# Two Mamba-2 layers and a quantised MLP on one core: the first convolution tap moves from GpSimd to ScalarE, with new instruction orders in the scan

## The chip, the core and the metric

The kernel runs on 1 core of one Trainium2 chip. The metric is the device time of one execution in microseconds; the time before is the median of 3 runs. The core has five instruction streams that run side by side and wait for each other by semaphores: TensorE (PE), VectorE (DVE), ScalarE (ACT), GpSimd (POOL) and SyncE (SP). Each runs its own instructions strictly in the order of the code.

## The reference

The input is x, 8 sequences of 1024 tokens of 256 channels. After a normalisation come two Mamba-2 layers with residuals, then x is added, normalised again, and three blocks of a quantised MLP with LoRA follow. The change touches the Mamba layers alone:

```python
zxbcdt = u @ in_w.T                       # u: layer norm of h; z 512, xBC 640, dt 8 columns
z, xBC, dt = split(zxbcdt)
dt = softplus(dt + dt_bias)
xBC = silu(causal_depthwise_conv(xBC, conv_w, 4 taps) + conv_b)
xh, B, C = split(xBC)                     # 512, 64, 64
dA = exp(dt * -exp(A_log))
state = dA * state + (dt * x) B^T ; y = state C      # per head, token after token
y = (y + D * xh) * silu(z)
y = y * rsqrt(mean(y * y) + eps) * rms_w
h = h + y @ out_w.T
```

## The kernel before

**Tiling.** A layer is worked off in 16 items; an item n is a chunk of 128 tokens of 4 of the 8 sequences, so 512 tokens. `over_items` (twice per layer by hand, then a hardware loop over pairs, then two by hand) runs the function `step(n, ...)` of each engine for the 32 items of both layers. The convolution works on tiles of 128 channels x 512 tokens in float32; there are five of them (`QCONV`), in the order B/C tile first, then four tiles of x, numbered i = 0 to 4. The scan within a chunk is done with matrix products: decays between tokens (`decays`, `exp_decay`, `weigh`, in four pieces k = 0 to 3, two blocks of tokens by half the heads), scores of C and B, the output within the chunk (`within`) and from the carried state (`carried`), and the new state (`new_state`).

**Staging.** In step(n) the engines finish item n and make the front part of item n + 1 (projections, convolution, softplus, its pieces k = 0 and 1) and the layer norm and transposes of item n + 2. No planner runs: the order of work on each engine is the order of the calls in its `step`, written out by hand, and each call begins with waits for semaphores that count instructions of other engines.

**A convolution tile i passes four engines.** TensorE's `project_conv(i)` (L502) makes it in a PSUM bank: two banks (`front`) alternate, so tile i needs that tile i - 2 is through. ScalarE's `raw_conv(i)` (L806) copies it with its bias to `xpad` in SBUF, behind a halo of 3 tokens which VectorE's `set_halo` (L1270) puts there. GpSimd's `first_tap(i)` (L1019) multiplies `xpad`, shifted by three tokens, with the weight of tap 0 into `xc`. VectorE's `convolve(i, 0..2)` (L1286) adds the other three taps; the first of them, `convolve(i, 0)`, waits for the first tap (`tap0`), each other one for the one before. ScalarE's `silu_conv(i)` (L824) ends it.

**The work around it.** ScalarE: `exp_decay(k)` (L851, Abs then Exp over two banks `dbank`), `exp_carry(pair)` (L864, Exp over the two `mix` banks), `softplus` (L797, with a table load for Ln), `norm` (L777), `square(t)` (L868), `silu_z(t)` (L846), `keep_b`, `double_c` (two DMAs on ScalarE's queue). VectorE: `layer_moments` (L1106), `bias_dt` (L1209), `weigh(k)` (L1309), `scale_x(b)` (L1318, frees the `mix` banks of `turn_x`), `scale_c(pair)` (L1323), `skip(t)` (L1329), `split_sums` (L1226, which makes the parts that `turn_cum` transposes), `decay_operands` (L1256), `first_operands` (L1264), `rest_u` (L1205), `mean_square` (L1346), `finish` (L1350). TensorE: `decays(k)` waits for `weigh(k - 1)`, since there is one pair of decay banks; `carry(0)` waits for all four `scale_x`, `carry(1)` for `scale_c(0)`; `outputs(0)` for `weigh(3)`; `project_conv(4)` for `convolve(2, 2)`; `turn_cum` (L522) for `convolve(4, 2)`; `project_z(t)` (L530) for `silu_z(t - 2)`. GpSimd: `to_end` (L1028), `gate(t)` (L1014, waits for `skip(t)`), `decay_state`, `layer_norm` (L983), `add_squares`, `second_operands` (L991), `norm_residual` (first layer alone), two `rsqrt`.

## Time and profile before

| | before |
|---|---|
| median of 3 runs | 1781.3 us (1776.38 to 1782.0) |
| profiled execution | 1781.56 us |
| its span, first to last instruction | 1779.8 us |
| TensorE busy | 1637.6 us, 92% |
| VectorE busy | 1369.8 us, 77% |
| ScalarE busy | 1268.5 us, 71% |
| GpSimd busy | 1183.8 us, 67% |
| mean granted TensorE clock | 0.978 |

The Mamba layers take the first 1370 us or so, the MLP the rest. Shares of busy time are means over parts with different limits, so the profile is read by the timeline: each row of it is an instruction or several of one kind in a run, with its start from the span's start, its length (of the whole run, where it is several), the engine, the line, what it writes and reads, and, in brackets, how long the engine had been idle before it and what released it. TensorE instructions overlap in their records. On the other engines a following instruction that depends on nothing may start about 0.1 us before the end of the one before.

### The profile page before, as it was taken

What the parts mean: (1) busy time and instruction counts of PE and PEld (TensorE: products, weight loads), DVE (VectorE), ACT (ScalarE), POOL (GpSimd) and SP (SyncE); (2) the same over time, 40 slices, a digit from 0 to 9 for tenths busy, and PEclk for the clock granted to TensorE, in tenths of its full rate; (3) what the DMA queues carried; (4) which work ended last, traced back from release to release, by engine and by line L of the source; (5) the groups of instructions that cost most, each with busy time, mean ns of one, the idle gap of its engine ahead of it and who ended that gap; (6) DMA issues with size and microseconds to landing.
All of it is one profiled execution on the core that took longest, in us unless ns stands there. A gap on an engine that the chain in (4) does not pass through costs nothing. (4 is left out here: it accounts for less than half of the span.)

```text
span 1779.8 us, 35344 instructions
## 1 busy us (share of the span) xinstructions
PE 1637.6 (92%) x12440; PEld 1290.7 (73%) x12440; DVE 1369.8 (77%) x2941; ACT 1268.5 (71%) x1999; POOL 1183.8 (67%) x1022
## 2 busy tenths in 40 slices
...
GB/s 162 19 48 43 43 41 41 56 62 41 41 41 47 41 42 36 48 43 43 43 53 64 41 41 41 47 41 41 29 160 32 99 1 143 1 109 35 36 13 48
DMA packets 87045, 91.67 MB, mean 52 GB/s; under 512 B 4928, under 2 KB 82224, under 8 KB 86960
## 3 DMA queue, kind: packets, MB, share of 16 engines
...
## 5 line engine op out<-in xcount | busy, mean ns | idle before, releaser
L1025 POOL TENSOR_TENSOR L_xc<-L_xpad,L_vec 128x512 f32<-128x512 f32 x160 | 166.2, 1039 | 313.2 <-ACT L_xpad L814 237.2
L498 PE MATMUL L_front<-L_uhi,L_whi 128*128 128x512 f32 x568 | 243.8, 429 | 9.2 <-DVE L_xc L1302 4.7
L666 PE MATMUL L_mix<-L_wo,L_yg 128*128 128x256 f32 x1024 | 240.7, 389 | 0.0
L853 ACT ACTIVATE L_dbank<-L_dbank 128x1024 f32<-128x1024 f32 x128 | 129.2, 1009 | 143.9 <-PE L_dbank L559 143.1
L498 PE MATMUL L_front<-L_uhi,L_wlo 128*128 128x512 f32 x568 | 226.4, 399 | 0.0
L498 PE MATMUL L_front<-L_ulo,L_whi 128*128 128x512 f32 x568 | 225.7, 397 | 0.0
L1315 DVE TENSOR_TENSOR L_m<-L_dbank,L_gm 128x1024 f32<-128x1024 f32 x128 | 156.3, 1221 | 84.2 <-ACT L_dbank L855 84.2
L666 PEld LDWEIGHTS L_mix<-L_wo,L_yg 128*128 128x128 f32 x1024 | 196.5, 195 | 28.7 <-issue 0.9
L1017 POOL TENSOR_TENSOR L_yg<-L_yg,L_sz 128x512 f32<-128x512 f32 x128 | 176.8, 1392 | 37.7 <-DVE L_yg L1331 37.7
L1036 POOL TENSOR_TENSOR L_wx<-L_dtx,L_decay 128x512 f32<-128x512 f32 x120 | 124.1, 1045 | 94.5 <-DVE L_dtx L1320 94.5
L1777 POOL TENSOR_TENSOR M_alo<-M_hT,M_ahi 128x512 fp32r<-128x512 f32 x96 | 129.3, 1362 | 46.3 <-ACT M_ahi L1710 46.3
L814 ACT ACTIVATE L_xpad<-L_front,L_pbias 128x512 f32<-128x512 f32 x156 | 106.6, 684 | 63.4 <-PE L_front L498 62.8
L498 PEld LDWEIGHTS L_front<-L_uhi,L_whi 128*128 128x128 f32 x568 | 108.0, 190 | 59.8 <-DVE L_xc L1302 19.3
L849 ACT ACTIVATE L_sz<-L_front,L_pbias 128x512 f32<-128x512 f32 x128 | 87.5, 685 | 85.8 <-PE L_front L498 82.2
L855 ACT ACTIVATE L_dbank<-L_dbank 128x1024 f32<-128x1024 f32 x128 | 129.0, 1008 | 3.4
L617 PE MATMUL L_ybank<-L_m,L_dtx 128*64 128x128 f32 x2048 | 129.4, 280 | 1.3 <-DVE L_m L1315 1.3
L1784 POOL TENSOR_TENSOR M_alo<-M_g,M_ahi 128x512 fp32r<-128x512 f32 x96 | 126.5, 1337 | 3.7 <-ACT M_ahi L1734 3.6
L1002 POOL TENSOR_TENSOR L_sq<-L_sq 128x512 f32<-128x512 f32 x96 | 124.6, 1298 | 3.7 <-ACT L_sq L870 0.5
L498 PEld LDWEIGHTS L_front<-L_uhi,L_wlo 128*128 128x128 f32 x568 | 108.0, 190 | 25.8
L617 PEld LDWEIGHTS L_ybank<-L_m,L_dtx 128*64 128x64 f32 x2048 | 113.6, 140 | 15.1 <-issue 12.0
L1296 DVE SCALAR_TENSOR_TENSOR L_front<-L_front,L_vec,L_xc 128x512 f32<-128x512 f32 x156 | 117.6, 754 | 5.2 <-POOL L_xc L1025 5.1
L498 PEld LDWEIGHTS L_front<-L_ulo,L_whi 128*128 128x128 f32 x568 | 108.6, 191 | 17.3
...
## 6 DMA issues: line engine op xcount, KB each, us to landing
...
```

The source lines that it names most:

```text
L498: last = nc.tensor.matmul(to[:, :], ww[:, kd, tile * P:(tile + 1) * P], a[:, kd, :], start=i == 0, stop=i == len(passes) - 1)
L617: nc.tensor.matmul(ybank[t % 2][half, b * P:(b + 1) * P], dtx[:, b, 2 * t + odd, :], m[:, b, 2 * t + odd, :], start=b == 0, stop=False, sk ...
L666: last = nc.tensor.matmul(mix[1 - s][:, (b % 2) * DM:(b % 2 + 1) * DM], yg[:, t, b * P:(b + 1) * P], wo[layer][:, t, :], start=t == 0, sto ...
L853: nc.scalar.activation(dbank[:, :, :], dbank[:, :, :], ACT.Abs).then_inc(d_abs, 1)
L855: nc.scalar.activation(dbank[:, :, :], dbank[:, :, :], ACT.Exp, scale=-1.0).then_inc(d_exp, 1)
L1002: nc.gpsimd.tensor_tensor(sq[:, 0, :], sq[:, 0, :], sq[:, t, :], ALU.add).then_inc(sq_added, 1)
L1017: nc.gpsimd.tensor_tensor(yg[:, t, :], yg[:, t, :], sz[:, t, :], ALU.mult).then_inc(y_gated, 1)
L1025: nc.gpsimd.tensor_tensor(xc[p][:, q, :].rearrange("p (b i) -> p b i", b=NB), xpad[:, q, :, 0:P], vector(layer, "conv_w", q * TAPS, 1).uns ...
L1036: nc.gpsimd.tensor_tensor(wx[:, b, :, :], dtx[:, b, :, :], decay[p][:, b, :].unsqueeze(2).broadcast_to([P, NH, HD]), ALU.mult).then_inc(wx ...
L1315: nc.vector.tensor_tensor(m[:, at, heads, :], dbank[:, :, :].rearrange("p b (h i) -> p b h i", i=P), gm[:, at, :].unsqueeze(2).broadcast_t ...
L1777: nc.gpsimd.tensor_tensor(alo[u][:, kd, :], hT[u][:, kd, :], ahi[u][:, kd, :].bitcast(F32), ALU.subtract).then_inc(h_lo, 1)
L1784: nc.gpsimd.tensor_tensor(alo[u][:, kd, :], g[u][:, kd, :], ahi[u][:, kd, :].bitcast(F32), ALU.subtract).then_inc(g_lo, 1)
```

## The change

The multiplication by the weight of tap 0 is no longer done on GpSimd. `first_tap` becomes an activation of ScalarE (Identity with a scale of one value per partition, SBUF to SBUF), called right behind `raw_conv` of the same tile, in the prologue too. It waits for the raw copy to be complete, and for tile 0 for `set_halo`. The other engines' waits stay. All four `step` functions get a new order:

- TensorE: `decays(2)` and `turn_dt` come before `result(n-1, 1)`; `project_conv(1)` and `decays(3)` before `turn_x(1)`; `carry(1)` behind `project_conv(3)`; `square_sums` behind `result(n, 0)`.
- ScalarE: `exp_decay(3)` before `keep_b`; `softplus` before `raw_conv(3)`; `norm` and `square(0)`, `square(1)` behind the second and third `silu_conv`; `square(2)` before `silu_z(1)`; `exp_sums` and `keep_halo` change places.
- GpSimd: `decay_state` before the gates, `layer_norm` behind `gate(1)`, `second_operands` behind the first `add_squares`, the `rsqrt` of the result before `norm_residual`.
- VectorE: `set_halo` behind `layer_moments`; `bias_dt` and `weigh(n, 2)` before `convolve(0, 0)`; `convolve(1, 2)` before `scale_c(0)`; `finish_dt` before `convolve(3, 0)`; `decay_operands` before `skip(2)`; `first_operands` before `add_state`; `mean_square` behind `rest_u`.

The diff (leading spaces cut):

```diff
@@ -713,26 +713,25 @@
     more, more2 = follows(n, 1), follows(n, 2)
     if more:
         project_conv(n + 1, 0)
+    spread_factors(n, 0)
+    turn_x(n, p, 0)
+    if more:
+        turn_dt(n + 1)
+    decays(n, 2)
     if follows_any(n):
         result(n - 1, layer_of(n, layer, -1), 1)
-    spread_factors(n, 0)
-    turn_x(n, p, 0)
-    decays(n, 2)
-    if more:
-        turn_dt(n + 1)
+    if more:
+        project_conv(n + 1, 1)
+    decays(n, 3)
     turn_x(n, p, 1)
     turn_x(n, p, 2)
-    if more:
-        project_conv(n + 1, 1)
     turn_x(n, p, 3)
     turn_b(n, p)
     carry(n, 0)
-    decays(n, 3)
     if more:
         project_conv(n + 1, 2)
+        project_conv(n + 1, 3)
     carry(n, 1)
-    if more:
-        project_conv(n + 1, 3)
     outputs(n, p, 0)
     spread_factors(n, 1)
     spread_factors(n, 2)
@@ -756,13 +755,13 @@
         scores(n + 1, 1 - p)
     if more2:
         turn_u(n + 2, p)
+    result(n, layer, 0)
+    if not more:
+        square_sums(n)
     if more:
         square_sums(n)
     if starts_layer(n + 2):
         fold_bias(layer_of(n, layer, 2))
-    result(n, layer, 0)
-    if not more:
-        square_sums(n)
     if more:
         decays(n + 1, 1)
     if more2:
@@ -821,6 +820,15 @@
     nc.scalar.activation(halo[g][:, :, :, :].rearrange("p q b i -> p (q b) i"),
                          xpad[:, :, :, P:P + HALO].rearrange("p q b i -> p (q b) i"), ACT.Copy).then_inc(halo_kept, 1)
 
+def first_tap(n, layer, p, i):
+    q = QORDER[i]
+    act.wait_ge(x_raw, QCONV * n + i + 1)
+    if i == 0:
+        act.wait_ge(halo_set, n + 1)
+        wait(act, y_skip, T * (n - 1))
+    nc.scalar.activation(xc[p][:, q, :].rearrange("p (b i) -> p b i", b=NB), xpad[:, q, :, 0:P], ACT.Identity,
+                         scale=vector(layer, "conv_w", q * TAPS, 1)).then_inc(tap0, 1)
+
 def silu_conv(n, layer, p, i):
     q = QORDER[i]
     act.wait_ge(taps, 3 * QCONV * n + 3 * i + 3)
@@ -891,6 +899,7 @@
     softplus(n)
     for i in range(QCONV):
         raw_conv(n, 0, p, i)
+        first_tap(n, 0, p, i)
     keep_halo(n, p)
     for i in range(QCONV):
         silu_conv(n, 0, p, i)
@@ -914,52 +923,56 @@
         raw_conv(n + 1, layer1, 1 - p, 0)
     exp_decay(n, 2)
     if more:
+        first_tap(n + 1, layer1, 1 - p, 0)
         raw_conv(n + 1, layer1, 1 - p, 1)
+        first_tap(n + 1, layer1, 1 - p, 1)
+    exp_decay(n, 3)
     keep_b(n)
     exp_carry(n, 0)
-    exp_decay(n, 3)
     if more:
         raw_conv(n + 1, layer1, 1 - p, 2)
+        first_tap(n + 1, layer1, 1 - p, 2)
     exp_carry(n, 1)
     round_mlp(n, 0)
     if more:
+        softplus(n + 1)
         raw_conv(n + 1, layer1, 1 - p, 3)
-        softplus(n + 1)
+        first_tap(n + 1, layer1, 1 - p, 3)
         silu_conv(n + 1, layer1, 1 - p, 0)
         raw_conv(n + 1, layer1, 1 - p, 4)
-    if more2:
-        norm(n + 2, p)
-    if more:
+        first_tap(n + 1, layer1, 1 - p, 4)
         silu_conv(n + 1, layer1, 1 - p, 1)
+        silu_conv(n + 1, layer1, 1 - p, 2)
+        double_c(n + 1, 1 - p)
     square(n, 0)
-    if more:
-        silu_conv(n + 1, layer1, 1 - p, 2)
     square(n, 1)
     round_mlp(n, 1)
     round_mlp(n, 2)
-    if more:
+    if more2:
+        norm(n + 2, p)
+    if more:
+        silu_conv(n + 1, layer1, 1 - p, 3)
+        silu_conv(n + 1, layer1, 1 - p, 4)
         silu_z(n + 1, layer1, 0)
-        silu_conv(n + 1, layer1, 1 - p, 3)
-        double_c(n + 1, 1 - p)
+    square(n, 2)
+    if more:
         silu_z(n + 1, layer1, 1)
-    square(n, 2)
-    if more:
         silu_z(n + 1, layer1, 2)
     square(n, 3)
     round_mlp(n, 3)
     round_mlp(n, 4)
     round_mlp(n, 5)
     if more:
-        silu_conv(n + 1, layer1, 1 - p, 4)
         silu_z(n + 1, layer1, 3)
         exp_decay(n + 1, 0)
+    if more2:
+        round_u(n + 2)
+    if more:
+        keep_halo(n + 1, 1 - p)
         exp_sums(n + 1, 1 - p)
     if starts_layer(n + 2):
         fold_weights(layer_of(n, layer, 2))
-    if more2:
-        round_u(n + 2)
-    if more:
-        keep_halo(n + 1, 1 - p)
+    if more:
         exp_decay(n + 1, 1)
 
 act.dma_start(raw[:, :, :], w["in_proj"][0].rearrange("(k p) n -> p k n", p=P)).then_inc(raw_in, 16)
@@ -1016,15 +1029,6 @@
     pool.wait_ge(z_done, T * n + T)
     nc.gpsimd.tensor_tensor(yg[:, t, :], yg[:, t, :], sz[:, t, :], ALU.mult).then_inc(y_gated, 1)
 
-def first_tap(n, layer, p, i):
-    q = QORDER[i]
-    pool.wait_ge(x_raw, QCONV * n + i + 1)
-    if i == 0:
-        pool.wait_ge(halo_set, n + 1)
-        wait(pool, y_skip, T * (n - 1))
-    nc.gpsimd.tensor_tensor(xc[p][:, q, :].rearrange("p (b i) -> p b i", b=NB), xpad[:, q, :, 0:P],
-                            vector(layer, "conv_w", q * TAPS, 1).unsqueeze(2).broadcast_to([P, NB, P]), ALU.mult).then_inc(tap0, 1)
-
 def to_end(n, p, b):
     if not stays(n):
         return
@@ -1050,39 +1054,27 @@
     more, more2 = follows(n, 1), follows(n, 2)
     layer1, next_layer = layer_of(n, layer, 1), layer_of(n, layer, 1)
     twice = layer_of(n, layer, 2) == 0
-    if more:
-        first_tap(n + 1, layer1, 1 - p, 0)
     to_end(n, p, 0)
     to_end(n, p, 1)
-    if more:
-        first_tap(n + 1, layer1, 1 - p, 1)
     to_end(n, p, 2)
+    to_end(n, p, 3)
+    decay_state(n, p)
+    gate(n, 0)
+    gate(n, 1)
     if more2:
         layer_norm(n + 2)
-    if more:
-        first_tap(n + 1, layer1, 1 - p, 2)
-    to_end(n, p, 3)
-    if more:
-        first_tap(n + 1, layer1, 1 - p, 3)
-        first_tap(n + 1, layer1, 1 - p, 4)
-    gate(n, 0)
-    gate(n, 1)
-    decay_state(n, p)
     gate(n, 2)
-    if more:
-        add_squares(n, 1)
     gate(n, 3)
-    if not more:
-        add_squares(n, 1)
+    add_squares(n, 1)
+    if more:
+        second_operands(n + 1)
     add_squares(n, 2)
     add_squares(n, 3)
+    if twice:
+        model_norm(n + 2, p)
+    rsqrt(rrms, ssq, ss_done, n, rr_done)
     if next_layer == 0:
         norm_residual(n + 1, c + p, 1 - p)
-    rsqrt(rrms, ssq, ss_done, n, rr_done)
-    if twice:
-        model_norm(n + 2, p)
-    if more:
-        second_operands(n + 1)
 
 for g in range(GROUPS):
     nc.gpsimd.memset(halo[g][:, :, :, :], 0.0)
@@ -1094,8 +1086,6 @@
 last.then_inc(cleared, 1)
 layer_norm(1)
 model_norm(1, 1)
-for i in range(QCONV):
-    first_tap(0, 0, 0, i)
 pool.wait_ge(consts_ready, 3)
 second_operands(0)
 norm_residual(0, 0, 0)
@@ -1394,31 +1384,29 @@
     more, more2 = follows(n, 1), follows(n, 2)
     layer1, layer2 = layer_of(n, layer, 1), layer_of(n, layer, 2)
     chunk2 = 0 if ends_sequence(n) else c + 1
-    if more:
-        set_halo(n + 1, 1 - p)
     if more2:
         layer_moments(n + 2, layer2, chunk2, p)
+    if more:
+        set_halo(n + 1, 1 - p)
+        bias_dt(n + 1, layer1)
+    weigh(n, 2)
     if more:
         convolve(n + 1, layer1, 1 - p, 0, 0)
     if follows_any(n):
         finish(n - 1, layer_of(n, layer, -1), None, 1 - p, 1)
     scale_x(n, p, 0)
     if more:
-        bias_dt(n + 1, layer1)
+        convolve(n + 1, layer1, 1 - p, 0, 1)
     scale_x(n, p, 1)
-    if more:
-        convolve(n + 1, layer1, 1 - p, 0, 1)
     scale_x(n, p, 2)
     if more:
         convolve(n + 1, layer1, 1 - p, 0, 2)
     scale_x(n, p, 3)
-    weigh(n, 2)
     if more:
         convolve(n + 1, layer1, 1 - p, 1, 0)
         convolve(n + 1, layer1, 1 - p, 1, 1)
+        convolve(n + 1, layer1, 1 - p, 1, 2)
     scale_c(n, 0)
-    if more:
-        convolve(n + 1, layer1, 1 - p, 1, 2)
     weigh(n, 3)
     if more:
         convolve(n + 1, layer1, 1 - p, 2, 0)
@@ -1427,11 +1415,12 @@
     if more:
         convolve(n + 1, layer1, 1 - p, 2, 1)
         convolve(n + 1, layer1, 1 - p, 2, 2)
+        finish_dt(n + 1, layer1, 1 - p)
         convolve(n + 1, layer1, 1 - p, 3, 0)
-        finish_dt(n + 1, layer1, 1 - p)
         convolve(n + 1, layer1, 1 - p, 3, 1)
+    skip(n, layer, p, 0)
+    if more:
         convolve(n + 1, layer1, 1 - p, 3, 2)
-    skip(n, layer, p, 0)
     skip(n, layer, p, 1)
     merge(n, 1)
     keep_rest(n, 0)
@@ -1441,10 +1430,11 @@
         convolve(n + 1, layer1, 1 - p, 4, 1)
         split_sums(n + 1)
         convolve(n + 1, layer1, 1 - p, 4, 2)
+        decay_operands(n + 1)
     skip(n, layer, p, 2)
-    if more:
-        decay_operands(n + 1)
     skip(n, layer, p, 3)
+    if more:
+        first_operands(n + 1)
     add_state(n, p, 0)
     add_state(n, p, 1)
     merge(n, 3)
@@ -1456,17 +1446,15 @@
     if ends_sequence(n) and more2:
         clear_halo(n, p)
     if more:
-        first_operands(n + 1)
         mask_scores(n + 1)
-    mean_square(n)
-    keep_rest(n, 4)
-    if more:
         weigh(n + 1, 0)
     if starts_layer(n + 2):
         fold_rows(layer2)
     if more2:
         rest_u(n + 2, 0)
         rest_u(n + 2, 1)
+    mean_square(n)
+    keep_rest(n, 4)
     finish(n, layer, c, p, 0)
     keep_rest(n, 5)
     if starts_layer(n + 2):
```

## Rows read from the trace of the kernel before

**Rows 1.** Stretches, second layer: busy us (x instructions) by engine, clock, DMA, GB/s

```profile
900.00:1000.00 100.00, 95.88 (x825) 74.30 (x826) 79.17 (x155) 77.57 (x119) 63.44 (x54) 1.00 0.13 39
```

**Rows 2.** Timeline of TensorE, an item's first part: start, us, engine, operation, idle before

```profile
777.65 0.41 PE L597 MATMUL L_mix<-L_dmov,L_sel 64*64 64x512 bf16 x4 [0.68 <-DVE L_cs L1326]
...
778.22 0.50 PE L498 MATMUL L_front<-L_uhi,L_whi 128*128 128x512 f32 x1 [0.15 <-DVE L_xc L1302]
...
779.80 1.97 PE L617 MATMUL L_ybank<-L_m,L_dtx 128*64 128x128 f32 x32
```

**Rows 3.** Timeline of VectorE, one item of the second layer

```profile
764.93 1.23 DVE L1315 TENSOR_TENSOR L_m<-L_dbank,L_gm 128x1024 f32<-128x1024 f32 x1 [1.43 <-ACT L_dbank L855]
...
768.23 0.75 DVE L1296 SCALAR_TENSOR_TENSOR L_front<-L_front,L_vec,L_xc 128x512 f32<-128x512 f32 x1
...
770.27 0.18 DVE L1214 TENSOR_TENSOR L_dtraw<-L_front,L_dtb 128x32 f32<-128x32 f32 x1
...
776.29 1.22 DVE L1326 TENSOR_TENSOR L_cs<-L_mix,L_cc 128x1024 f32<-128x1024 f32 x1
...
777.42 0.73 DVE L1302 SCALAR_TENSOR_TENSOR L_xc<-L_xpad,L_vec,L_front 128x512 f32<-128x512 f32 x1
...
778.08 1.22 DVE L1315 TENSOR_TENSOR L_m<-L_dbank,L_gm 128x1024 f32<-128x1024 f32 x1
...
789.03 0.74 DVE L1302 SCALAR_TENSOR_TENSOR L_xc<-L_xpad,L_vec,L_front 128x512 f32<-128x512 f32 x1
...
804.98 1.23 DVE L1315 TENSOR_TENSOR L_m<-L_dbank,L_gm 128x1024 f32<-128x1024 f32 x1 [1.43 <-ACT L_dbank L855]
```

**Rows 4.** Timeline of VectorE, one item of the first layer

```profile
586.91 1.23 DVE L1315 TENSOR_TENSOR L_m<-L_dbank,L_gm 128x1024 f32<-128x1024 f32 x1 [1.43 <-ACT L_dbank L855]
...
611.16 0.74 DVE L1302 SCALAR_TENSOR_TENSOR L_xc<-L_xpad,L_vec,L_front 128x512 f32<-128x512 f32 x1
...
627.08 1.23 DVE L1315 TENSOR_TENSOR L_m<-L_dbank,L_gm 128x1024 f32<-128x1024 f32 x1 [1.43 <-ACT L_dbank L855]
```

**Rows 5.** Timeline of TensorE, the item's second part

```profile
789.93 0.28 PE L526 MATMUL L_front<-L_identb,L_cum 128*128 128x128 bf16 x2
...
794.38 0.39 PE L498 MATMUL L_front<-L_uhi,L_whi 128*128 128x512 f32 x1
...
802.47 0.39 PE L559 MATMUL L_dbank<-L_dmov,L_dstat 64*128 64x512 bf16 x2
```

**Rows 6.** Costliest groups: count, busy us, mean ns of one, idle before and releaser

```profile
L1025 POOL TENSOR_TENSOR L_xc<-L_xpad,L_vec 128x512 f32<-128x512 f32 x160 | 166.2, 1039 | 313.2 <-ACT L_xpad L814 237.2 <-DVE L_xpad L1278 75.9
...
L827 ACT ACTIVATE L_xc<-L_xc,L_cbias 128x512 f32<-128x512 f32 x160 | 114.0, 713 | 8.1 <-DVE L_xc L1302 7.8
...
L849 ACT ACTIVATE L_sz<-L_front,L_pbias 128x512 f32<-128x512 f32 x128 | 87.5, 685 | 85.8 <-PE L_front L498 82.2 <-issue 1.2 <-ACT L_xc L827 0.5
...
L870 ACT ACTIVATE L_sq<-L_yg 128x512 f32<-128x512 f32 x128 | 80.0, 625 | 12.4 <-POOL L_yg L1017 12.4
```

**Rows 7.** Timeline of ScalarE around softplus and norm

```profile
778.11 1.01 ACT L866 ACTIVATE L_mix<-L_mix 128x1024 f32<-128x1024 f32 x1
...
780.50 0.22 ACT L800 ACTIVATE L_dtabs<-L_dtraw 128x32 f32<-128x32 f32 x1
...
782.29 0.23 ACT L804 ACTIVATE L_dtln<-L_dtexp 128x32 f32<-128x32 f32 x1
...
785.03 2.07 ACT L780 ACTIVATE M_first<-M_first,L_shift,L_rstd 128x256 f32<-128x256 f32 x4
```

**Rows 8.** Timeline of GpSimd, two gates

```profile
790.87 1.29 POOL L1017 TENSOR_TENSOR L_yg<-L_yg,L_sz 128x512 f32<-128x512 f32 x1 [0.28 <-DVE L_yg L1331]
...
793.38 1.74 POOL L1017 TENSOR_TENSOR L_yg<-L_yg,L_sz 128x512 f32<-128x512 f32 x1
```

**Rows 9.** Timeline of VectorE behind turn_cum

```profile
791.02 0.41 DVE L1261 TENSOR_SCALAR L_dmovT<-L_front,M_kept 128x256 bf16<-128x256 bf16 x1
...
793.20 0.77 DVE L1267 TENSOR_TENSOR L_dmov<-L_dmovT,L_mask 128x1024 bf16<-128x1024 bf16 x1
```

More of the change, by code:

```diff
@@ L925, in step @@
                 if more:
+                    softplus(n + 1)
                     raw_conv(n + 1, layer1, 1 - p, 3)
-                    softplus(n + 1)
+                    first_tap(n + 1, layer1, 1 - p, 3)
                     silu_conv(n + 1, layer1, 1 - p, 0)
                     raw_conv(n + 1, layer1, 1 - p, 4)
+                    first_tap(n + 1, layer1, 1 - p, 4)
+                    silu_conv(n + 1, layer1, 1 - p, 1)
+                    silu_conv(n + 1, layer1, 1 - p, 2)
+                    double_c(n + 1, 1 - p)
+                square(n, 0)
+                square(n, 1)
+                round_mlp(n, 1)
+                round_mlp(n, 2)
                 if more2:
```

21 lines of the change are left out of this document (8 added, 13 removed).

## The prediction

> **What bounds the kernel now.** I read the table of stretches first, to see how full each engine is once the loop runs. TensorE is busy 96 of 100 us, VectorE 79, ScalarE 78 and GpSimd 63 [rows 1]. That looks like a TensorE bound with a few per cent of waits, and the change seems aimed at them. The timelines say something narrower. They must be read for where an item's time is set: I follow one item of the second layer, from one weigh(n,1) on VectorE to the next. Those two start at 764.93 and 804.98, so an item takes 40.05 us [rows 3].
>
> In the first part, VectorE sets the pace. From 764.93 to the end of the last tap of tile 4 (789.03 + 0.74 = 789.77) its timeline shows no idle time at all: 24.84 us of work without a gap [rows 3]. TensorE's turn_cum needs that tap and starts at 789.93 [rows 5]. Since a hand-over from VectorE to TensorE costs 0.07 us (a conv tap that starts at 777.42 and takes 0.73 ends at 778.15, and project_conv(3) starts at 778.22 [rows 2, 3]), VectorE has only 0.16 - 0.07 = 0.09 us to spare.
>
> In the second part, TensorE sets it: from turn_cum at 789.93 to decays(n+1,1) at 802.47 are 12.54 us of z projections, scores, transposes and result(n,0) [rows 5], and from there ScalarE's Abs and Exp lead back to weigh at 804.98, 2.51 us [rows 3, 5]. 25.00 + 12.54 + 2.51 = 40.05. In the first layer the same chain can be seen with a longer VectorE part: weigh starts at 586.91, the last tap at 611.16, 24.25 us against 24.10, because layer_moments has two more instructions there; and the item takes 627.08 - 586.91 = 40.17 us, 0.12 more [rows 3, 4]. So a tenth more on VectorE in this part is a tenth more per item. That is the row that decides: VectorE's full stretch is the bound, although its mean share is only 79%.
>
> TensorE's waits within that part, as the 0.68 us before carry(1) [rows 2], are waits for VectorE. They are a result of the bound and nothing that an order of TensorE can take away.
>
> **The change, part by part.** GpSimd loses five multiplications of 1.04 us an item [rows 6]. It waited for ScalarE before nearly all of them, and nothing else on it was late, so this gives nothing by itself. ScalarE gains five copies. Their price is not in the trace; the nearest row is silu_conv, SBUF to SBUF on the same 512 columns with one per-partition operand, 0.71 us. Square, without such an operand, takes 0.625 us [rows 6]; norm, with two of them, 2.07 / 4 = 0.52 for half the columns, which puts a full tile near 0.8 [rows 7]. I take 0.71, with 0.62 and 0.80 as ends. Each copy also waits for the raw copy before it to complete (0.68 + 0.03), where other work follows 0.1 us before the end. So ScalarE goes from 31 to about 34.5 us of 40, and only its place in the chain matters.
>
> The Trainium skill (ScalarE: Activation LUTs, What ACT_TABLE_LOAD costs) gives 280 ns plus 0.833 ns a column for an activation with one per-partition operand, 707 ns here. The silu row above agrees within 0.01 us.
>
> VectorE's set of instructions between weigh(n,1) and the last tap of tile 4 is the same as before; only its order is new. So this part can't get shorter than its 24.84 us. What counts is where the new order makes it wait. I go through it with w = 0 at the start of weigh(n,1); a VectorE instruction hands its engine on about 0.09 us before its end.
>
> 1. weigh(n,2) now comes right behind bias_dt. weigh(n,1), layer_moments and set_halo take 768.23 - 764.93 = 3.30 us, bias_dt 0.33 (two instructions of 0.18, the second waiting for the first) [rows 3]: VectorE is there at 3.63. Its input: decays(n,2) on TensorE waits for weigh(n,1) to free the bank, 1.23 + 0.05, and then 2.51 as above: 3.79. Idle: 0.16. In the first layer the two extra instructions (0.15) fill it.
> 2. turn_x(1) now stands behind result(n-1,1), project_conv(1) and decays(3). By adding the lengths it is done at 7.65, and VectorE wants it at 7.63. Idle: 0.02.
> 3. The three taps of tile 1 come one behind the other, before scale_c(0). A tap that waits for its predecessor has its whole 0.75 us and 0.03 of hand-over, 0.78 us, instead of 0.66 (777.42 to 778.08) [rows 3]. There are five such pairs instead of four: 0.12.
> 4. scale_c(1). carry(1) now stands behind project_conv(3), which needs the last tap of tile 1. From the end of that tap: 0.07, then project_conv 1.58 (778.22 to 779.80), carry to ScalarE 0.46 (777.65 to 778.11), Exp 1.01, hand-over 0.04: 3.16 us [rows 2, 7]. VectorE gets there after scale_c(0) 1.13, weigh(3) 1.14 and one tap 0.66, less 0.08 of overlap: 2.85 [rows 3]. Idle: 0.31.
> 5. The first tap of tile 3. On ScalarE it stands behind exp_carry(1), softplus and raw_conv(3). From the start of exp_carry(1): 0.92 (its 1.01 less the overlap), softplus with its table load 1.79 + 0.14 (780.50 to 782.29, then 0.14) [rows 7], raw copy and its wait 0.71, scaled copy 0.71, 0.03: 4.30 us. VectorE, from the same start: 1.05 until scale_c(1), which takes 1.13, two taps 0.78 + 0.67 and finish_dt 0.33: 3.96. Idle: 0.34. Before, this product sat on GpSimd and ScalarE did raw_conv(3) ahead of softplus; that cover is gone.
>
> Sum: 0.16 + 0.02 + 0.12 + 0.31 + 0.34 = 0.95, less the 0.09 to spare, 0.86 us an item; in the first layer 0.71.
>
> The second part: does TensorE run as smoothly from turn_cum (call it T) to decays(1)? result(n,0) and square_sums only change places. mean_square moves behind rest_u and is ready before VectorE gets to it; rsqrt and finish end some 0.2 us before weigh needs VectorE. norm now stands behind gate(0), gate(1) and GpSimd's layer_norm, so silu_z(0) ends at about T + 3.10, where project_z(2) wants it at T + 3.06: 0.04 us. And square(2) now stands ahead of silu_z(1), which project_z(3) needs; project_z(3) starts at 794.38, T + 4.45 [rows 5]. The chain is turn_cum and hand-over 0.33, decay_operands 0.64 (twice 0.41 less the overlap), skip(2) 0.75, 0.08, gate(2) 1.29, 0.04, square 0.52 (0.62 less the overlap), silu_z 0.685, 0.05: T + 4.39 [rows 5, 6, 8, 9]. It just fits. Total: 0.90 us an item in the second layer, 0.75 in the first.
>
> Fourteen items of each layer run like this: 14 x 0.90 + 14 x 0.75 = 23.1 us. For the three items at the borders I take 0.8 each, and 0.4 off in the prologue, where the first tap comes earlier: 2.0 us. MLP, weights and DMAs are as before. The profiled execution took 1781.56 us (span 1779.8), the median of the runs is 1781.3: 1781.6 + 25.1 = 1807 us.
>
> **The rivals.** (a) gate(2) is stretched. In the trace a gate takes 1.29 us, but 1.74 when first_operands (0.77 us, from 793.20) was already running on VectorE as it started [rows 8, 9]. The new order puts first_operands about half a us behind the start of gate(2) in every item. If gate(2) takes 1.74, silu_z(1) ends at T + 4.84 and project_z(3) waits 0.39: 14 x (1.25 + 1.10) + 2.0 = 34.9, 1816 us. For it: the overlap is certain, and the chain has 0.06 to spare. Against it: in the only rows that show a stretch, VectorE started first, here GpSimd does.
>
> The Trainium skill (SBUF — State Buffer, Who interferes with whom) says that a VectorE instruction with two SBUF inputs and a GpSimd instruction reading SBUF exclude each other, and the one that starts first keeps the port to its end. By that rule gate(2) keeps 1.29 us and 1807 stands; the 1.74 above agrees with it as far as it goes.
>
> (b) The waits on TensorE are what costs time, and the new order removes them: faster. If it did away with all idle time of TensorE in the loop, 4.1 us in 100 [rows 1], 28 items would give 28 x 1.64 = 46 us, 1736 us. It decides only if VectorE could be ahead of its 24.84 us by more than a tenth, and nothing moves out of that stretch. 6%.
>
> (c) The waits of steps 1 to 5 are absorbed, because several estimates are a few tenths too long at once (a scaled copy of 0.62, softplus cut short): no change, 1783 us. Steps 4 and 5 are sums of measured lengths of 3.16 and 4.30 us, in which 0.3 us is a tenth. 8%.
>
> (d) ScalarE becomes the bound: square, norm and silu_z queue up behind the added 3.6 us, project_z(1) to (3) each wait, and an item takes 1.7 us more: 14 x (1.7 + 1.55) + 2 = 1829 us. Against it: ScalarE still has 5 us free an item. 10%.
>
> **How the numbers follow.** Forecast 1807: 50%; (a) 26%; (d) 10%; (c) 8%; (b) 6%. The forecast's own bounds: a copy at 0.62 us and no idle in steps 1 and 2 leave 0.6 us an item, 1798; a copy at 0.80 and 0.1 more on ScalarE give 1.1, 1813. The range takes in (a) and part of (c) and (d): 1790 to 1825. A measurement of this kernel tells about 0.3% (5.3 us) from no change. Faster: 6%. Same: 8%. Slower: 86%.
>
> **What would show it.** In the profile of the changed kernel an item of the second layer should take about 40.95 us. VectorE should show gaps of 0.3 us before scale_c(1) (waiting for the Exp of both banks) and before the first tap of tile 3 (waiting for ScalarE's copy), and 0.16 before weigh(n,2) in the second layer only. conv copies should last 0.71 us. TensorE should still wait before a carry. project_z(3) waiting 0.4 us for ScalarE, with gate(2) at 1.74, shows (a). The forecast is wrong if the stretch from weigh(n,1) to the last tap of tile 4 is not about 25.7 us, or if turn_cum no longer follows it closely.

## Result, and the profile after

The changed kernel takes 1806.9 us (median of the runs, 1804.0 to 1810.2) against 1778.9 us (1776.4 to 1782.0) for the kernel before, measured beside it: a ratio of 1.0164 (95% interval 1.0133 to 1.0194), so 28 us slower (by the interval 24 to 35). The medians of the kernel before beside the experiments below are 1780.0 (19 runs), 1781.4 and 1781.7 (13 runs each); against those the rise is 25 to 27 us. Its profiled execution took 1803.97 us, span 1802.2, 22.4 us above the one of before.

| us of the profiled execution | before | after | difference |
|---|---|---|---|
| start to the first steady weigh(n,1) | 103.97 | 106.23 | +2.3 |
| 13 items of the first layer | 523.11 | 533.10 | +10.0, 0.77 an item |
| the three items at the border of the layers | 137.85 | 132.69 | -5.2 |
| 13 items of the second layer | 520.37 | 532.88 | +12.5, 0.96 an item |
| from there to the end | 494.50 | 497.30 | +2.8 |

Each line is the distance between two starts of weigh(n,1) on VectorE. The shares of the page after, where GpSimd's and ScalarE's parts of the change show and nothing else does:

```profile
PE 1657.5 (92%) x12440; PEld 1294.6 (72%) x12440; DVE 1400.4 (78%) x2941; ACT 1375.2 (76%) x2159; POOL 1021.4 (57%) x862
```

One item of the second layer on VectorE (timeline of after; columns: start, us, engine, line, operation, tiles, and the idle time before with its releaser). weigh is L1305, a conv tap L1286, L1289 or L1292, scale_c L1316, finish_dt L1211:

```profile
813.06 1.23 DVE L1305 TENSOR_TENSOR L_m<-L_dbank,L_gm 128x1024 f32<-128x1024 f32 x1 [0.24 <-ACT L_dbank L863]
...
816.62 0.19 DVE L1207 TENSOR_TENSOR L_dtraw<-L_front,L_dtraw 128x32 f32<-128x32 f32 x1
816.86 1.23 DVE L1305 TENSOR_TENSOR L_m<-L_dbank,L_gm 128x1024 f32<-128x1024 f32 x1
...
824.75 0.75 DVE L1292 SCALAR_TENSOR_TENSOR L_xc<-L_xpad,L_vec,L_front 128x512 f32<-128x512 f32 x1
...
828.64 1.22 DVE L1316 TENSOR_TENSOR L_cs<-L_mix,L_cc 128x1024 f32<-128x1024 f32 x1 [0.22 <-ACT L_mix L874]
...
831.45 0.19 DVE L1213 TENSOR_TENSOR L_da<-L_dtv,L_aneg 128x32 f32<-128x32 f32 x1
831.91 0.76 DVE L1286 SCALAR_TENSOR_TENSOR L_front<-L_front,L_vec,L_xc 128x512 f32<-128x512 f32 x1 [0.28 <-ACT L_xc L829]
...
838.09 0.74 DVE L1292 SCALAR_TENSOR_TENSOR L_xc<-L_xpad,L_vec,L_front 128x512 f32<-128x512 f32 x1
...
841.24 1.35 DVE L1257 TENSOR_TENSOR L_dmov<-L_dmovT,L_mask 128x1024 bf16<-128x1024 bf16 x1
...
853.99 1.23 DVE L1305 TENSOR_TENSOR L_m<-L_dbank,L_gm 128x1024 f32<-128x1024 f32 x1
```

The stretch that had no gap in [rows 3] now has two, before scale_c(1) and before the first tap of tile 3, and runs from 813.06 to 838.83: 25.77 us instead of 24.84. The item ends at 853.99 (40.93 us; its neighbours take 41.04, the mean of eight is 41.00). TensorE, as in [rows 2, 5], turn_cum (L526) and decays(n+1,1) (the L559 at 851.47):

```profile
823.64 0.41 PE L597 MATMUL L_mix<-L_dmov,L_sel 64*64 64x512 bf16 x4 [0.93 <-ACT L_bt L870]
...
827.89 1.97 PE L617 MATMUL L_ybank<-L_m,L_dtx 128*64 128x128 f32 x32 [0.34 <-DVE L_m L1305]
...
838.96 0.28 PE L526 MATMUL L_front<-L_identb,L_cum 128*128 128x128 bf16 x2 [0.32 <-DVE L_xc L1292]
...
851.47 0.39 PE L559 MATMUL L_dbank<-L_dmov,L_dstat 64*128 64x512 bf16 x2
```

turn_cum waits for the last tap, 0.13 us behind its end. From there to decays(1) it is 12.51 us (12.54 before) and to weigh another 2.52 (2.51 before). 25.77 + 0.13 + 12.51 + 2.52 = 40.93. TensorE still waits before carry(0), before the outputs and for the last tap; what was added to the item is in VectorE's stretch.

ScalarE and GpSimd around the two gaps and the gates (scaled copy L829, square L878, gate L1030, which is the last line), to be held against [rows 7, 8]:

```profile
827.60 1.01 ACT L874 ACTIVATE L_mix<-L_mix 128x1024 f32<-128x1024 f32 x1 [0.49 <-PE L_mix L597]
828.52 0.22 ACT L799 ACTIVATE L_dtabs<-L_dtraw 128x32 f32<-128x32 f32 x1
828.77 0.23 ACT L801 ACTIVATE L_dtexp<-L_dtabs 128x32 f32<-128x32 f32 x1
829.02 1.28 ACT L803 ACT_TABLE_LOAD   x1
830.32 0.23 ACT L803 ACTIVATE L_dtln<-L_dtexp 128x32 f32<-128x32 f32 x1
830.45 0.67 ACT L813 ACTIVATE L_xpad<-L_front,L_pbias 128x512 f32<-128x512 f32 x1
831.16 0.72 ACT L829 ACTIVATE L_xc<-L_xpad,L_vec 128x512 f32<-128x512 f32 x1
...
842.07 0.63 ACT L878 ACTIVATE L_sq<-L_yg 128x512 f32<-128x512 f32 x1
...
840.74 3.00 POOL L1030 TENSOR_TENSOR L_yg<-L_yg,L_sz 128x512 f32<-128x512 f32 x2 [2.70 <-DVE L_yg L1321]
```

From the start of exp_carry(1) to the tap that needs the scaled copy it is 831.91 - 827.60 = 4.31 us, without a pause on ScalarE.

### The profile page after: what moved, and what is told of

Same layout as the page of the kernel before. It is cut to its first block and busy times, and to the rows that moved or that the text cites. A ratio compares the mean times of both kernels' runs of the same rounds, so it can differ in the third digit from the quotient of the medians.

```text
span 1802.2 us, 35284 instructions
## 1 busy us (share of the span) xinstructions
PE 1657.5 (92%) x12440; PEld 1294.6 (72%) x12440; DVE 1400.4 (78%) x2941; ACT 1375.2 (76%) x2159; POOL 1021.4 (57%) x862
## 5 line engine op out<-in xcount | busy, mean ns | idle before, releaser
L1030 POOL TENSOR_TENSOR L_yg<-L_yg,L_sz 128x512 f32<-128x512 f32 x128 | 177.5, 1398 | 373.7 <-DVE L_yg L1321 372.5
L498 PE MATMUL L_front<-L_uhi,L_whi 128*128 128x512 f32 x568 | 248.2, 437 | 16.9 <-DVE L_xc L1292 9.3
L666 PE MATMUL L_mix<-L_wo,L_yg 128*128 128x256 f32 x1024 | 240.0, 388 | 0.0
L1305 DVE TENSOR_TENSOR L_m<-L_dbank,L_gm 128x1024 f32<-128x1024 f32 x128 | 156.4, 1222 | 86.7 <-ACT L_dbank L863 85.1
L666 PEld LDWEIGHTS L_mix<-L_wo,L_yg 128*128 128x128 f32 x1024 | 193.0, 193 | 32.6 <-issue 7.9
L1286 DVE SCALAR_TENSOR_TENSOR L_front<-L_front,L_vec,L_xc 128x512 f32<-128x512 f32 x156 | 117.5, 753 | 9.4 <-ACT L_xc L829 9.4
L1289 DVE SCALAR_TENSOR_TENSOR L_front<-L_xpad,L_vec,L_front 128x512 f32<-128x512 f32 x156 | 117.4, 752 | 3.4
L829 ACT ACTIVATE L_xc<-L_xpad,L_vec 128x512 f32<-128x512 f32 x160 | 115.6, 722 | 4.3
```

What stands on the lines that cost most here:

```text
L498: last = nc.tensor.matmul(to[:, :], ww[:, kd, tile * P:(tile + 1) * P], a[:, kd, :], start=i == 0, stop=i == len(passes) - 1)
L666: last = nc.tensor.matmul(mix[1 - s][:, (b % 2) * DM:(b % 2 + 1) * DM], yg[:, t, b * P:(b + 1) * P], wo[layer][:, t, :], start=t == 0, sto ...
L1030: nc.gpsimd.tensor_tensor(yg[:, t, :], yg[:, t, :], sz[:, t, :], ALU.mult).then_inc(y_gated, 1)
L1286: nc.vector.scalar_tensor_tensor(acc, acc, weight(3), to, ALU.mult, ALU.add).then_inc(taps, 1)
L1305: nc.vector.tensor_tensor(m[:, at, heads, :], dbank[:, :, :].rearrange("p b (h i) -> p b h i", i=P), gm[:, at, :].unsqueeze(2).broadcast_t ...
```

## The experiments

All times are medians with a run of the kernel before beside them; "item" is the mean distance of weigh(n,1) or weigh(n,2) over 8 to 12 items of the second layer (40.03 us before, 41.00 after).

### Is VectorE's stretch the bound? 0.7 us more in it, and 0.7 us in the gap

Both insert the same two instructions into the kernel before (0.74 us for the two in either trace), once ahead of weigh(n,2), once ahead of mask_scores.

```diff
+    if more:
+        dve.wait_ge(wo_ready, LAYERS)
+        for j in range(2):
+            nc.vector.bn_stats(idle[:, j, :], wo[1][:, j, :])
     weigh(n, 2)
```

> The kernel before, with two more VectorE instructions an item (bn_stats of 256 columns, about 0.35 us each, so 0.70 us), put ahead of weigh(n,2), inside the stretch that VectorE fills without a gap. Theory (that stretch sets the item): +0.70 less the 0.09 to spare, 0.61 us for each of 31 items, +19 us (1.1%). Rival (TensorE, 96% busy, is the bound and VectorE at 79% has room): 0 to +2 us. Nothing of the result is changed.

> The kernel before, with the same two VectorE instructions (0.70 us an item) put ahead of mask_scores, where VectorE waits 3.2 us for TensorE. Theory: 0 us (within 0.3%), the gap shrinks to 2.5 us. Rival (VectorE's total load counts): +19 us as in the other place.

In the stretch: 1809.2 us, ratio 1.0162 (1.0134 to 1.0191), +29 us. In the gap: 1779.7, ratio 0.9997 (0.9980 to 1.0015). So the same work of VectorE costs time ahead of weigh(n,2) and nothing in the gap, which is what the prediction's first part rests on. What the pads leave open is the rest of the stretch. The pad stands ahead of the third tap of tile 1. From project_conv(3), which that tap releases, TensorE too works without a pause up to turn_cum (778.22 to 789.93, 11.71 us in [rows 2, 5]; with the pad 958.24 to 969.97, 11.73). So behind that tap both engines are full, TensorE is the later of the two by the 0.09 us of the prediction, and no pad was put there.

The item is as expected: most went up by 0.65 us (0.61 expected). The kernel's +29 is more than the +19 expected. Five of 14 items of the second layer took about 1.5 us more than before (mean item 40.9), and of the 29.0 us between the profiled executions 7.5 lie outside the 26 items of the table above. The timeline of TensorE shows such a long item, and the table of stretches the granted clock (columns: us, busy us (x instructions) of PE, PEld, DVE, ACT and POOL, PEclk, DMA share, GB/s):

```profile
911.87 0.41 PE L598 MATMUL L_mix<-L_dmov,L_sel 64*64 64x512 bf16 x4 [0.65 <-ACT L_bt L863]
913.50 0.47 PE L560 MATMUL L_dbank<-L_dmov,L_dstat 64*128 64x512 bf16 x2 [1.23 <-DVE L_m L1316]
913.90 0.79 PE L499 MATMUL L_front<-L_uhi,L_whi 128*128 128x512 f32 x1
```

```profile
900.00:905.00 5.00, 5.00 (x24) 3.54 (x23) 3.56 (x8) 3.19 (x4) 0.89 (x2) 1.00 0.00 0
911.00:914.00 3.00, 1.12 (x9) 0.34 (x7) 3.00 (x6) 1.46 (x3) 2.85 (x3) 0.95 0.65 162
914.00:917.00 3.00, 3.00 (x10) 1.85 (x10) 2.96 (x5) 2.15 (x3) 0.35 (x2) 0.50 0.55 188
```

TensorE idles 0.65 and then 1.23 us, and for the 3 us behind that the granted clock is 0.50, the lower of its two levels (1.2 GHz); the item takes 41.51 us. But the same two waits, 0.57 to 0.65 and 1.22 to 1.33 us, stand in all 14 items, and in the other nine the six matmuls of 512 columns behind them keep the spacing of full clock. So in five items the waits cost more than their length; what tells those five from the others is not shown.

### The two halves: the tap on ScalarE in the old order, and the new orders with the tap on GpSimd

The first replaces GpSimd's first_tap by the one on ScalarE and leaves all orders. The second is the changed kernel with first_tap back on GpSimd:

```diff
@@ tap only, against before: ScalarE (GpSimd's five calls are taken out)
     raw_conv(n + 1, layer1, 1 - p, 0)
+    first_tap(n + 1, layer1, 1 - p, 0)
...
@@ orders only, against after: GpSimd (ScalarE's five calls are taken out)
+    first_tap(n + 1, layer1, 1 - p, 0)
     to_end(n, p, 0)
+    first_tap(n + 1, layer1, 1 - p, 1)
     to_end(n, p, 1)
     to_end(n, p, 2)
     to_end(n, p, 3)
+    first_tap(n + 1, layer1, 1 - p, 2)
     decay_state(n, p)
+    first_tap(n + 1, layer1, 1 - p, 3)
+    first_tap(n + 1, layer1, 1 - p, 4)
```

> The kernel before with one part of the change alone: the first tap on ScalarE right behind the raw copy, all orders as they were (GpSimd's calls of it just left out). Theory: the copy behind raw_conv(1) delays keep_b and exp_decay(3), so exp_carry(1) ends 1.0 us later and scale_c(1) waits 0.3; softplus is 0.7 later and the first tap of tile 4 waits 0.2; with the copies behind each other about +0.6 us an item, +17 us (1.0%), at most +25. Rival (the new orders alone cost the time, the tap is free): within 5 us of before. Rival (the load on ScalarE alone costs it): as much as the whole change, +28 us.

> The changed kernel with the first tap back on GpSimd (called there between to_end and the gates), all new orders kept. Theory: the first tap of tile 3 comes 0.4 us later than from ScalarE, and the gates on GpSimd, behind tile 4's tap, push layer_norm, norm and silu_z(0) back by 1.3 us, so project_z(2) waits too: an item 1.3 to 2.3 us longer than before, +38 to +70 us over before. Rival (what costs is ScalarE's added load): it takes the time back, within 10 us of before.

Tap only: 1787.9, ratio 1.0049 (1.0033 to 1.0064), +8 us, item 40.40. Right in sign, half of what was expected: scale_c(1) starts 0.89 us behind the tap before it instead of 0.66, and the first tap of tile 4 waits 0.18. Orders only: 1824.5, ratio 1.0237 (1.0196 to 1.0278), +45 us, item 41.53, within the 1.3 to 2.3 us more that were expected: the orders alone are worse than the whole change. Timelines of VectorE and GpSimd with the orders alone:

```profile
923.92 1.22 DVE L1321 TENSOR_TENSOR L_cs<-L_mix,L_cc 128x1024 f32<-128x1024 f32 x1 [0.22 <-ACT L_mix L865]
...
926.50 1.06 DVE L1216 SCALAR_TENSOR_TENSOR L_dtv<-L_dtraw,L_dtln 128x32 f32<-128x32 f32 x1
...
927.71 0.76 DVE L1291 SCALAR_TENSOR_TENSOR L_front<-L_front,L_vec,L_xc 128x512 f32<-128x512 f32 x1
...
933.89 0.74 DVE L1297 SCALAR_TENSOR_TENSOR L_xc<-L_xpad,L_vec,L_front 128x512 f32<-128x512 f32 x1
```

```profile
926.48 1.04 POOL L1023 TENSOR_TENSOR L_xc<-L_xpad,L_vec 128x512 f32<-128x512 f32 x1 [2.14 <-ACT L_xpad L813]
```

The first tap of tile 3 (927.71) starts 3.79 us behind scale_c(1); in after it is 3.27 (828.64 to 831.91). Of these 0.52 us, 0.36 are the product itself, which GpSimd ends at 927.52: the tap could not start before 927.55. That is the 0.4 that was expected. The other 0.16 is finish_dt, 0.18 us of work in after (831.23), which takes 1.06 here, to 0.04 us behind the end of that product, which began 0.02 us before it. The second half of the expectation, gates that push back norm and silu_z(0), did not happen: from the last tap of tile 4 (its end at 934.63) to the next weigh(n,1) at 949.80 it is 15.17 us, and 15.16 in after. The gap before scale_c(1) is there with the tap on either engine. So in the new orders the move to ScalarE gives back 0.5 us an item, and in the old one it costs 0.4. The two halves don't add.

### Undoing steps 5 and 4, one at a time and together

```diff
@@ ScalarE, step 5
-    softplus(n + 1)
     raw_conv(n + 1, layer1, 1 - p, 3)
     first_tap(n + 1, layer1, 1 - p, 3)
+    softplus(n + 1)
...
@@ VectorE, step 5
-    finish_dt(n + 1, layer1, 1 - p)
     convolve(n + 1, layer1, 1 - p, 3, 0)
+    finish_dt(n + 1, layer1, 1 - p)
```

> The changed kernel with step 5 undone: softplus behind the scaled copy of tile 3 again, and finish_dt between the first two taps of tile 3 again. Theory: the 0.28 us wait before that tap goes, 0.04 comes in before finish_dt; 0.24 us less in each of 31 items, 7 us less than the changed kernel, so about +20 us over the kernel before (1.1%). Rival (the load on ScalarE and not the place in the order): no difference from the changed kernel, +28 us.

1801.9, ratio 1.0106 (1.0074 to 1.0139), item 40.86. The time is the one expected (+20 us), the item is not: 0.14 us less where 0.24 was expected. The gap before tile 3 is gone, but one before tile 4 takes its place:

```profile
908.79 1.22 DVE L1316 TENSOR_TENSOR L_cs<-L_mix,L_cc 128x1024 f32<-128x1024 f32 x1 [0.20 <-ACT L_mix L874]
...
915.43 0.76 DVE L1286 SCALAR_TENSOR_TENSOR L_front<-L_front,L_vec,L_xc 128x512 f32<-128x512 f32 x1 [0.32 <-ACT L_xc L829]
```

```diff
@@ TensorE, step 4
     project_conv(n + 1, 2)
-    project_conv(n + 1, 3)
     carry(n, 1)
+    project_conv(n + 1, 3)
...
@@ VectorE, step 4
-    convolve(n + 1, layer1, 1 - p, 1, 2)
     scale_c(n, 0)
+    convolve(n + 1, layer1, 1 - p, 1, 2)
```

> The changed kernel with step 4 undone: carry(1) ahead of project_conv(3) and scale_c(0) ahead of the third tap of tile 1. Theory: the 0.22 us wait before scale_c(1) goes, but scale_c(0) now waits 0.5 us for exp_carry(0), which the new order puts behind exp_decay(3) and keep_b; the third tap and project_conv(3) come later by as much. Net 0 to +0.2 us an item against the changed kernel: +28 to +34 us over before. Rival (each wait is a loss of its own, so to undo its cause gives it back): 0.22 less an item, +21 us.

1798.6, ratio 1.0090 (1.0058 to 1.0121), item 40.76: 0.24 us less. The theory had 0 to 0.2 us more and is wrong; its rival had 0.22 less. The wait before scale_c(0) came as the theory said, and the item still got shorter. Both gaps of after are gone, and one of 0.42 stands before scale_c(0):

```profile
902.42 1.22 DVE L1317 TENSOR_TENSOR L_cs<-L_mix,L_cc 128x1024 f32<-128x1024 f32 x1 [0.42 <-ACT L_mix L875]
...
915.09 0.74 DVE L1293 SCALAR_TENSOR_TENSOR L_xc<-L_xpad,L_vec,L_front 128x512 f32<-128x512 f32 x1
916.41 0.41 DVE L1252 TENSOR_SCALAR L_dstat<-L_front,M_kept 128x256 bf16<-128x256 bf16 x1 [0.58 <-PE L_front L526]
```

What I had left out: exp_carry(1) is also the head of ScalarE's run to the tap of tile 3 (4.31 us). With carry(1) earlier it starts 13.98 us behind weigh(n,1) instead of 14.54, so step 5's gap goes with step 4's. The stretch falls from 25.77 to 25.50.

> The kernel after, with both undo's at once: carry(1) and scale_c(0) back in their old places, and softplus and finish_dt behind tap 3. Alone the first brought the item from 41.0 to 40.76 us and the second to 40.88. Theory: the gaps before scale_c(1) and before the first tap of tile 3 are one and the same delay of ScalarE met twice, so the second undo adds nothing once the first is made: the item stays at 40.7 to 40.8 us and the time at 1798 us (1.009 to 1.010 of before). Rival 1: they are two delays that add: item 41.0 - 0.24 - 0.12 = 40.64, 1807 - 8.3 - 5 = 1793.5 us. Rival 2 (the prediction's own sum, steps 4 and 5 at 0.65): 1807 - 0.65 x 28 = 1789 us.

1808.5, ratio 1.0153 (1.0119 to 1.0186), item 41.10: together the two undo's give nothing, and all three expectations were wrong. ScalarE's timeline has the reason:

```profile
868.58 1.01 ACT L875 ACTIVATE L_mix<-L_mix 128x1024 f32<-128x1024 f32 x1
870.30 0.69 ACT L814 ACTIVATE L_xpad<-L_front,L_pbias 128x512 f32<-128x512 f32 x1 [0.72 <-PE L_front L498]
871.02 0.72 ACT L830 ACTIVATE L_xc<-L_xpad,L_vec 128x512 f32<-128x512 f32 x1
...
876.31 0.72 ACT L830 ACTIVATE L_xc<-L_xpad,L_vec 128x512 f32<-128x512 f32 x1
```

Now project_conv(3) runs behind carry(1), and ScalarE, with softplus behind raw_conv(3), waits 0.72 us for it; with step 5 as in the change softplus filled that wait. From exp_carry(1) to the end of the copy of tile 4 it is 8.45 us here against 7.73 with step 4 alone undone (904.31 to 912.04), and VectorE waits 0.42 before scale_c(0) and 0.31 before tile 4. So step 5 is a loss beside carry(1) late and a gain beside carry(1) early.

### Can 2.1 us come out of the stretch? layer_moments one step earlier

```diff
@@ VectorE
-    layer_moments(n + 2, layer2, chunk2, p)
...
+    if follows(n, 3):
+        layer3 = layer_of(n, layer, 3)
+        layer_moments(n + 3, layer3, c + 1 + p - CHUNKS * (layer3 - layer), 1 - p)
     if more:
         mask_scores(n + 1)
```

It moves 2.1 us (814.21 to 816.36 in after) from the stretch into the gap; for it one more pair of items per layer of VectorE's code stands outside the hardware loop. It was done to the kernel before, to the one with the tap on ScalarE, and to the one with both undo's. A fourth kernel has it, the tap on ScalarE, and an order written by the prediction's steps (decays(2) behind turn_dt, turn_x(1) behind project_conv(1), carry(1) behind project_conv(3), the taps of tile 0 and weigh(n,2) ahead of finish(n-1,1), finish_dt between the taps of tile 3); it also puts the second and third tap of tile 2 ahead of scale_c(1).

> The kernel before with layer_moments (2.06 us of VectorE an item) made one step earlier, in the gap in which VectorE waits 3.2 us for the scores; what the first layer needs of the model's own norm (two small instructions) stays. Theory in detail: VectorE's stretch loses 2.06 us of work, but finish(n-1,1) right behind it waits for result(n-1,1) on TensorE, which ends only 0.14 us before finish started; so the gap just moves and an item gains 0.13 us: -4 us (0.2%). Rival (the length of VectorE's stretch alone counts): 2.06 less an item until TensorE is the bound, -45 us or more.

> The kernel before with the taps on ScalarE (old orders, item 40.4 to 40.5 us) and layer_moments one step earlier. With the moments moved and the tap still on GpSimd, VectorE waited 1.29 us for GpSimd's product of tile 0 and the item was 39.95. On ScalarE that product comes earlier. Theory: TensorE binds within 0.3 us: item 39.7 to 40.0, 1768 to 1778 us, ratio 0.993 to 0.999. Rival 1: VectorE alone sets the stretch: 40.4 - 2.1 = 38.3, about 1730 us. Rival 2: ScalarE's copies hold up carry and the first taps whatever VectorE does: item stays at 40.4, 1788 us.

> after_both with layer_moments (2.1 us on VectorE) done one step earlier, in VectorE's gap behind finish, so that the stretch from weigh(n,1) to the last tap of tile 4 has 2.1 us less to do. Theory: TensorE stands close behind VectorE; from the end of scale_c(1) it needs 8.3 us (outputs, project_conv(4), states, sums, outputs) to turn_cum, and in the kernel before, with the same change, only 0.1 us an item was won. So the item falls to about 40.0 us and no lower than 39.8: 1776 to 1782 us, ratio 0.996 to 1.000. Rival: VectorE alone sets the stretch in this order: item 40.7 - 2.1 = 38.6, about 1740 us.

> A new order made with this theory: layer_moments one step earlier as in before_early, first taps on ScalarE, and turn_x(0), bias_dt, all three taps of tile 0 and weigh(n,2) placed ahead of finish(n-1,1), so that VectorE has work while TensorE makes result(n-1,1); turn_x(1) right behind project_conv(1); project_conv(2) ahead of carry(0); exp_carry(1) ahead of the scaled copy of tile 3 and that ahead of softplus. Theory: VectorE's stretch is 24.84 - 2.06 us of work, 0.3 for taps behind each other, 0.9 waiting for turn_x(1), 0.3 elsewhere: 24.3, an item 39.5 us instead of 40.05, -17 us (1%), between -25 and 0. Rival (TensorE's waits move elsewhere, since it is 96% busy): no faster than before.

- Kernel before: 1777.1, ratio 0.9977 (0.9964 to 0.9990), item 39.95. As expected, and the only kernel here that is faster than the one before. Of 2.1 us, 0.08 an item is won in the second layer and 0.24 in the first (39.94 against 40.18). VectorE now waits 1.29 us for GpSimd's product of tile 0, and behind that tap 0.42 for TensorE's result(n-1,1), without which finish can't start: the wait that was expected. finish starts 3.81 us behind weigh(n,1) instead of 3.96.
- Tap on ScalarE: 1784.7, ratio 1.0022 (1.0004 to 1.0040), item 40.25. Expected was 39.7 to 40.0 and, by the second rival, 40.4: it lies between, nearer to the rival. It wins 0.15 of 2.1 in the second layer, 0.29 in the first. Here too VectorE waits for result(n-1,1), 0.84 us, and finish starts at 3.81.
- Both undo's: 1807.6, ratio 1.0143 (1.0104 to 1.0181), item 41.09 against 41.10 without: nothing. Expected was about 40.0.
- The order by steps: 1802.3, ratio 1.0116 (1.0091 to 1.0141), item 40.67, +21 us where -17 was expected.

The lines are, in this order, VectorE at the first tap of tile 0 and at finish (early moments alone), at finish (with the tap on ScalarE), VectorE at weigh(n,2) (both undo's), and TensorE at the outputs and at turn_cum (order by steps):

```profile
923.28 0.76 DVE L1303 SCALAR_TENSOR_TENSOR L_front<-L_front,L_vec,L_xc 128x512 f32<-128x512 f32 x1 [1.29 <-POOL L_xc L1026]
924.46 0.88 DVE L1366 SCALAR_TENSOR_TENSOR L_hres<-L_mix,L_rrms,L_hres 128x256 f32<-128x256 f32 x2 [0.42 <-PE L_mix L667]
```

```profile
887.96 0.88 DVE L1361 SCALAR_TENSOR_TENSOR L_hres<-L_mix,L_rrms,L_hres 128x256 f32<-128x256 f32 x2 [0.84 <-PE L_mix L667]
```

```profile
858.96 1.23 DVE L1313 TENSOR_TENSOR L_m<-L_dbank,L_gm 128x1024 f32<-128x1024 f32 x1 [2.14 <-ACT L_dbank L865]
```

```profile
915.81 1.10 PE L625 MATMUL L_ybank<-L_cs,L_state 64*64 64x128 f32 x32 [1.02 <-issue]
...
924.04 0.29 PE L527 MATMUL L_front<-L_identb,L_cum 128*128 128x128 bf16 x2
```

In the new order weigh(n,2) comes third, and its input is not there before 3.8 us behind weigh(n,1), by decays(2) and ScalarE's Abs and Exp. The moments had filled just that wait: taken out, VectorE waits 2.14 us and starts at the same place. In the order by steps the second half of outputs(n,0) starts 0.10 us behind scale_c(1), which ends at 915.71; from there TensorE has 8.33 us of work without a pause (outputs, project_conv(4), states, sums, outputs) up to turn_cum, so a late scale_c(1) is a late turn_cum, whatever VectorE has left to do. VectorE's stretch is thus a bound with four others within a few tenths of a microsecond: result(n-1,1) in the old order (0.15 us before finish wants it), weigh(n,2)'s input in the new one, ScalarE's run from exp_carry(1), and TensorE's 8.3 us behind scale_c(1).

## Why the prediction was right, by its steps

**The bound.** Right for the changed kernel: turn_cum follows the last tap in after, the stretch is 25.77 us where about 25.7 was expected, and the item 41.00 where 40.95 was. The pads show it for the kernel before up to the third tap of tile 1; behind that tap the bound is shared with TensorE, which is the later one by 0.09 us. What the prediction did not have is how near the others are; for a change that only adds waits this did no harm, for the experiments that take work out it is what the expectations lacked.

**Step 1.** weigh(n,2) starts 3.80 us behind weigh(n,1) (3.88 in every other item), expected 3.79. In the first layer VectorE is busy up to it (598.28 to 602.15), as expected. **Steps 2 and 3.** The last tap of tile 1 ends 12.44 us behind weigh(n,1); about 12.4 follows from the prediction's lengths. **Step 4.** From there to scale_c(1) it is 3.14 us, expected 3.16. **Step 5.** From exp_carry(1) to the first tap of tile 3 it is 4.31, expected 4.30, with a scaled copy of 0.72 where 0.71 was taken. The gaps in brackets are 0.05, 0.22 and 0.28 instead of 0.16, 0.31 and 0.34, but they aren't the same measure: a bracket counts from the end of the instruction before, the prediction from 0.09 us ahead of that end, where VectorE can hand on. Counted like the prediction's they are 0.14, 0.31 and 0.37. The sum is right too: 25.77 against 24.84 + 0.95 = 25.79. The undo's show that both causes are real, and that steps 4 and 5 are not independent, as the sum has them. Neither adding the two undo's (1793.5 or 1789 us) nor taking the gaps as one delay (1798) gave the 1808.5 of both together.

**Second part.** Right: 12.51 us. decays(n+1,1) comes no later behind turn_cum than before; the hand-over to turn_cum is 0.13 instead of 0.07. The mean item is 41.00 and not 40.93 as this one, because every other item has weigh(n,2) at 3.88 and takes about 41.04.

**Rival (a).** gate(2) was not stretched: it runs from 840.74, and the square that needs it starts at 842.07. first_operands, from 841.24, takes 1.35 us instead of the 0.77 in [rows 9]: VectorE is held up, in a place where nothing waits for it. This is what the Trainium skill (SBUF — State Buffer, Who interferes with whom) says of a VectorE instruction with two SBUF inputs behind a GpSimd one, and the trace agrees: 1.35 here, and 1.06 for finish_dt with the orders alone. gate(3), which begins while first_operands is running, is the stretched one: the two gates take 3.00 us together, and two without first_operands beside them 2.60 (834.20 in the same trace). The square behind gate(3) doesn't wait for it. Of the 1.5 us an item that the orders alone cost, 0.16 is put down to finish_dt above.

**Rivals (b), (c), (d).** TensorE's waits were not removed; no step was absorbed; ScalarE went to 76% of the span and is late in the two places of steps 4 and 5, and what follows the z projections (decays(n+1,0), 6.04 us behind turn_cum against 5.94 before) comes 0.1 us later, which is made up before decays(n+1,1).

**The sum.** 0.77 an item in the first layer against 0.75, 0.96 against 0.90 in the second. Mis-sized is the term for the borders, 2.0 us. Beside the 26 items of the table the rest comes to -0.1: prologue and end cost 2.3 + 2.8, and the border between the layers gains 5.2. By the prediction's count of 28 items it is 22.4 - 14 x 0.77 - 14 x 0.96 = -1.8, so 3.8 us off, and the items are 1.1 above their 23.1. TensorE at the border, before, then after (L470 is fold_bias, L666 a result, L485 the first projection of dt with the folded weights):

```profile
661.45 7.47 PE L470 MATMUL L_ybank<-L_vec,L_raw 128*128 128x1 f32 x36 [0.35 <-DVE L_ssq L1348]
...
669.64 6.58 PE L666 MATMUL L_mix<-L_wo,L_yg 128*128 128x256 f32 x16
...
680.22 0.61 PE L485 MATMUL L_front<-L_uhi,L_wdt 128*16 128x512 f32 x1 [3.67 <-DVE L_wlo L1142]
```

```profile
673.54 3.62 PE L666 MATMUL L_mix<-L_wo,L_yg 128*128 128x256 f32 x16
...
678.49 6.24 PE L470 MATMUL L_ybank<-L_vec,L_raw 128*128 128x1 f32 x36 [0.55 <-DVE L_ssq L1338]
...
686.06 0.61 PE L485 MATMUL L_front<-L_uhi,L_wdt 128*16 128x512 f32 x1
```

Before, result(n,0) stood behind fold_bias; finish and fold_rows came late, and TensorE waited 3.67 us for the folded weights, at a clock of 0.63 in 660 to 680. The new order puts the result first, which I had read as a mere change of places with square_sums. That this is the whole of the 5.2 us was not tried by itself. The median of the runs rose by 28.0 us, the profiled executions by 22.4; the forecast's 25.1 lies between, and inside the interval of 24 to 35. That 1807 was met within 0.1 us is luck: the scatter of the runs alone is 6 us, and the border term was off by 3.8.
